# Attention stage of an audio tower kernel: another order of the softmax and query work in a step

## What is computed

```
q = rmsnorm(rope(x @ wq.T)) * q_norm_w        # 16 heads, x is the layer norm of h
k = rmsnorm(rope(x @ wk.T)) * k_norm_w        # 1 head
v = x @ wv.T
attn = softmax(mask(q @ k.T / 8))             # causal, 128 rows by 128 columns, per head
h = h + (attn @ v) @ wo.T
rmsnorm(x) = x * rsqrt(mean(x * x over the 64 values) + eps)
```

## Time and profile before

| | |
|---|---|
| time, median of 3 runs | 1922.25 us (1918.28 to 1922.78) |
| the profiled execution, its own time | 1921.04 us |
| its span | 1919.1 us |
| TensorE matmul (PE) busy | 1778.8 us, 93% |
| TensorE weight load (PEld) busy | 1275.9 us, 66% |
| VectorE (DVE) busy | 1530.7 us, 80% |
| ScalarE (ACT) busy | 1355.5 us, 71% |
| GpSimd (POOL) busy | 920.5 us, 48% |

### The profile page before, as it was taken

How to read it: one execution, slowest core, us unless ns; L and a number is a source line. 1 busy time by engine, 2 the same in 40 slices (tenths; PEclk the granted TensorE clock), 3 DMA queues, 4 the chain that set the end, 5 groups by cost and what they waited for, 6 DMA issues and landing times.

```text
span 1919.1 us, 35529 instructions
## 1 busy us (share of the span) xinstructions
PE 1778.8 (93%) x10789; PEld 1275.9 (66%) x10789; DVE 1530.7 (80%) x3377; ACT 1355.5 (71%) x3865; POOL 920.5 (48%) x1544
## 2 busy tenths in 40 slices
PE   3999999999999977999997999999999999989998
PEld 2777887887887866877775666666655665654443
DVE  5788888888888856567657899998999888986665
ACT  1567777677677653444445999999998999986765
POOL 1222322322322310032238999999898999983200
PEclk9999999999999988999997999999999999999999
DMA  3311111111111000000000000000000000004454
GB/s 98 95 44 40 34 45 39 34 45 39 34 45 39 25 1 1 1 1 1 1 1 1 2 2 2 2 2 2 2 2 1 2 2 2 2 7 177 189 216 165
DMA packets 30520, 69.05 MB, mean 36 GB/s; under 512 B 14108, under 2 KB 14748, under 8 KB 28028
## 3 DMA queue, kind: packets, MB, share of 16 engines
q1 hardware_dynamic: 30332, 66.78, 10.6%
HBM read 45.12 MB, written 2.36 MB: 25 GB/s over the span
## 4 chain that ended last, share of the span: by engine, by line
PE 33%; DVE 10%; ACT 9%; issue 6%; POOL 4%; DVEq 0%; ACTq 0%; POOLq 0%
ACT apb L1460 5%; PE ps L65 4%; PE ps L67 3%; PE ps L66 3%; PE ps L1218 3%; PE ps L1777 3%; PE ps L1201 3%; PE ps L1189 3%; PE ps L1228 2%; POOL apb L1574 1%; DVE atq L1281 1%; PE ps L1763 1%; PE ps L1184 1%; DVE amx L1321 1%; ACT aqT L1449 1%
## 5 line engine op out<-in xcount | busy, mean ns | idle before, releaser
L1460 ACT ACTIVATE apb<-ps,amx 128x128 f32<-128x128 f32 x1024 | 360.5, 369 | 23.6 <-DVE amx L1321 22.8
L1574 POOL TENSOR_TENSOR apb<-apb,arc 128x512 f32<-128x512 f32 x256 | 268.2, 1048 | 28.4 <-DVE arc L1329 27.4
L1460 ACT ACTIVATION_READ_ACCUMULATOR apb<-ps,amx 128x1 f32 x1024 | 214.4, 209 | 0.0
L1336 DVE COPY apT<-ps 128x512 f32<-128x512 f32 x256 | 172.6, 674 | 51.2 <-PE ps L1201 47.9
L583 POOL TENSOR_TENSOR h0h<-h0h,const 128x1 fp32r<-128x1 f32 x256 | 46.7, 218 | 338.8 <-DVE h0l L479 338.8
L65 PE MATMUL ps<-h0h,w123h 128*128 128x512 f32 x512 | 203.2, 397 | 0.0
L67 PE MATMUL ps<-h0h,w123l 128*128 128x512 f32 x512 | 202.5, 396 | 0.0
L66 PE MATMUL ps<-h0l,w123h 128*128 128x512 f32 x512 | 202.5, 395 | 0.0
L479 DVE SCALAR_TENSOR_TENSOR h0l<-ps,h0h 128x1024 fp32r<-128x1024 f32 x128 | 156.1, 1219 | 46.5 <-ACT h0h L383 46.5
L1201 PEld LDWEIGHTS ps<-const,apb 128*128 128x128 f32 x1024 | 109.8, 141 | 121.3 <-issue 90.9
L1321 DVE TENSOR_REDUCE amx<-ps 128x4 f32<-128x512 f32 x256 | 174.3, 681 | 4.6 <-PE ps L1189 4.3
(11 more groups left out here) (325 smaller groups left out, 5030.8 us busy)
## 6 DMA issues: line engine op xcount, KB each, us to landing
h<-gates SPq DMA_DIRECT2D x8, 2048.0 KB, 7.0
atq<-gates SPq DMA_DIRECT2D x8, 2048.0 KB, 7.0
x0k<-x0h SPq DMA_DIRECT2D x128, 72.0 KB
x<-in_x SPq DMA_DIRECT2D x32, 192.0 KB, 2.6
x0k<-x0l SPq DMA_DIRECT2D x64, 72.0 KB
x0k<-x0h SPq DMA_DIRECT2D x64, 48.0 KB
out<-akT SPq DMA_DIRECT2D x16, 128.0 KB, 1.9
x0k<-x0l SPq DMA_DIRECT2D x32, 48.0 KB
```

What stands on the lines that cost most here:

```text
L1336: ve.tensor_copy(pT[:, 4 * k:4 * k + 4, :], ps[:, TB, :].rearrange("p (h t) -> p h t", h=4)).then_inc(S["pT"], 1)
L1460: last = ac.activation(pb[:, i % 2, head, :], ps[:, SB[n % 3], h * T:(h + 1) * T], ACT.Exp, bias=mx[:, k, h:h + 1], accum_out=sm[:, i % 2, ...
L1574: po.tensor_tensor(p, p, rc[:, i % 2, 4 * k:4 * k + 4].unsqueeze(2).to_broadcast([T, 4, T]), ALU.mult).then_inc(S["pn"], 1)
```

## The change

- Slots of `rms_q` and `scale_q`: `rms_q` is called once per item, over all 16 heads, in slot `4 i - 7`. `scale_q` comes two slots later than before, one slot ahead of `q_t`.
- `square` reads the rotated sum `qr` from SBUF (and waits for `add_q`), no longer the bank QB. So `project`, which overwrites QB, waits for the rotation and not for the square.
- VectorE: in an even slot both maxima of the step; in an odd slot `recip(u - 1)`, `rope_q`, `recip(u)`, `sum_q` (two slots after its `rope_q`), then `p_copy`.
- ScalarE: in an odd slot `exps(u)` comes first; in an even slot `exps(u)` comes after the copies and ahead of `keep_x` and `square`.

```diff
-    at_rms = by_slot(HALVES, lambda m: 4 * (m // 2) - 9 + 2 * (m % 2))
-    at_qm = by_slot(HALVES, lambda m: 4 * (m // 2) - 8 + 2 * (m % 2))
+    at_rms = by_slot(B, lambda i: 4 * i - 7)
+    at_qm = by_slot(HALVES, lambda m: 4 * (m // 2) - 6 + 2 * (m % 2))
...
             if m >= 1:
-                pe.wait_ge(S["sq"], m)
+                pe.wait_ge(S["rope"], m)
...
             if i >= 1:
-                ve.wait_ge(S["lrq"], m - 1)
+                ve.wait_ge(S["lrq"], i)
...
-            if 0 <= u < PARTS:
-                maximum(u)
-            if 0 <= u - 1 < PARTS:
-                recip(u - 1)
+            if u % 2 == 0:
+                if 0 <= u < PARTS:
+                    maximum(u)
+                    maximum(u + 1)
+            else:
+                if 0 <= u - 1 < PARTS:
+                    recip(u - 1)
+                if u in at_q:
+                    rope_q(at_q[u])
+                if 0 <= u < PARTS:
+                    recip(u)
+                if u - 2 in at_q:
+                    sum_q(at_q[u - 2])
             if u in at_pt:
                 p_copy(at_pt[u])
-            if u in at_q:
-                rope_q(at_q[u])
-            if u - 1 in at_q:
-                sum_q(at_q[u - 1])
...
-            ac.wait_ge(S["rope"], m + 1)
+            ac.wait_ge(S["qr"], m + 1)
             if i >= 1:
                 ac.wait_ge(S["ssq"], m - 1)
-            ac.activation(sqb[:, h, :], ps[:, QB, :], ACT.Square).then_inc(S["sq"], 1)
-
-        def rms_q(m):
-            i, h = m // 2, m % 2
-            heads = slice(8 * h, 8 * h + 8)
-            ac.wait_ge(S["ssq"], m + 1)
-            ac.activation(lrq[:, heads], ssq[:, heads], ACT.Ln, bias=epsc[:, 1:2], scale=1.0 / DH
-                          ).then_inc(S["lrq"], 1)
-            ac.wait_ge(S["lrq"], m + 1)
+            ac.activation(sqb[:, h, :], qr[i % 2][:, h, :], ACT.Square).then_inc(S["sq"], 1)
+
+        def rms_q(i):
+            ac.wait_ge(S["ssq"], 2 * i + 2)
+            ac.activation(lrq[:], ssq[:], ACT.Ln, bias=epsc[:, 1:2], scale=1.0 / DH).then_inc(S["lrq"], 1)
+            ac.wait_ge(S["lrq"], i + 1)
             if i >= 1:
-                ac.wait_ge(S["qm"], m - 1)
-            ac.activation(rq[:, heads], lrq[:, heads], ACT.Exp, scale=-0.5).then_inc(S["rq"], 1)
+                ac.wait_ge(S["qm"], 2 * i)
+            ac.activation(rq[:], lrq[:], ACT.Exp, scale=-0.5).then_inc(S["rq"], 1)
...
+            if u % 2 == 1 and 0 <= u < PARTS:
+                exps(u)
             if u - 1 in at_pv:
                 keep_o(at_pv[u - 1])
-            if u - 1 in at_q:
-                square(at_q[u - 1])
             if u - 1 in at_qt:
                 keep_q(at_qt[u - 1])
             if u in at_rms:
                 rms_q(at_rms[u])
-            if u in at_xt:
-                keep_x(at_xt[u])
...
-            if 0 <= u < PARTS:
+            if u % 2 == 0 and 0 <= u < PARTS:
                 exps(u)
+            if u in at_xt:
+                keep_x(at_xt[u])
+            if u - 1 in at_q:
+                square(at_q[u - 1])
...
-            po.wait_ge(S["rq"], m + 1)
+            po.wait_ge(S["rq"], m // 2 + 1)
```

## The result

The changed kernel takes 2002.27 us (median of 4 runs, 1998.03 to 2003.35) against 1921.39 us for the kernel before, timed beside it: ratio 1.0419, 95% interval 1.0399 to 1.0439. It is 81 us slower. The forecast was 1972 us, +50; the result lies 0.7 us inside the upper end of the range of 1926 to 2003.

The account below looks back on a forecast made before the run. A new ring of VectorE and ScalarE waits was to bind each attention step at 5.46 us. Groups of 43.68 + 2.55 + 0.2 + 0.2 = 46.63 us against 43.30 gave +46.6, the tail +4: 1972 us, range 1926 to 2003.

Parts of the forecast that it names:

- the ring: VectorE and ScalarE, attention steps: maximum, exponentials(e), square, exponentials(o), reciprocal(o), `p_copy`, `sum_q`, next maximum; 5.46 us per step; chance 0.72.
- a fall of the clock in every group: TensorE in the step with `statistics`: idling lowers its clock, +1.6 us per group, +23 in all, 1995 us; chance 0.08.
- What is put into the ring: VectorE and ScalarE: `residual` 0.79, `statistics` 0.93, `keep_x` 0.50, `sum_k` 0.33 lengthen their steps, 2.55 us per group.
- Scores have 1.9 us in hand, and the excess of 2 x 0.51 goes into that: TensorE in the two `w_o` steps: spare time before scores absorbs their excess; 0.2 us per group, ends 0 and 1.0.
- the transposes ahead of `p_copy` have less in hand: TensorE in the `w_o` steps: these transposes have less spare time than scores; 0.2 us per group taken.
- Bounded by that 0.5 us of slack turning into 0 to 0.3 per step: GpSimd: cost if it fell behind with `add_q` or the later `scale_q`; 0 to 0.3 us per step.
- The square from SBUF at 0: ScalarE: square reading SBUF instead of PSUM changes the step by -0.03 to +0.06 us; taken at 0.
- The ends: Outside the 14 regular groups: nothing ahead of 1057 us, +4 us in the 63 us behind, ends 0 and 10.
- The saved pair and the `project` wait at nothing: ScalarE's saved Ln and Exp lie in a gap, and TensorE was not late by `project`'s wait; no gain from either.
- Faster: VectorE reaches reciprocal(o) after its exponentials end, so no wait binds there; 1902 us; chance 0.12.
- No change: Attention steps: 5.36 us, with `residual`, `statistics` and `keep_x` finding cover; 1924 us; chance 0.07.
- The clock falling in every step: TensorE: idling lowers its clock in every step, 112 times +4.7 us, up to 2500 us; chance 0.01.

Follow-up runs that it names:

- the edit that puts 0.5 us into it: Changed kernel with `keep_o` ahead of the exponentials in odd slots: 2039.85 us, ratio 1.0626.
- `scale_q` first: Changed kernel with `scale_q` ahead of `normalize` in GpSimd's order, nothing else: 1988.81 us, ratio 1.0353.
- the pair per half: Changed kernel with the root-mean-square pair again once per half item, pair and scaling in the slots of before: 1988.76 us, ratio 1.0359.
- both rings open, `keep_o` first: Changed kernel, odd reciprocal a slot later, `keep_o` ahead of odd exponentials, plus pair once per half item (1937.06 us) or `scale_q` ahead of `normalize` (1942.36 us).

## Why the forecast was right, and why too small

The direction and the mechanism held. That the time fell inside the range was luck: the ring's own range ended at 1996, and what lies above was room for a fall of the clock in every group, which came in one. The 30.3 us that were missing are in terms taken too small, below.

**The ring: right, in five of the eight steps.** 5.44 against 5.46, and the edit that puts 0.5 us into it lengthens the steps by that. In the steps with `rope_k` and `w_o` other things last longer: VectorE's own list and TensorE's matmuls.

**What is put into the ring: right.** `residual` with `keep_y`, `statistics`, `keep_x`, `sum_k`: 6.47, 6.39, 5.95, 5.79 against 6.45, 6.39, 5.96, 5.79. `rope_k` was costed at nothing and took 0.08: in that step the reciprocals no longer wait, and VectorE's own list is 5.54 long. That `sum_k` came out to the hundredth in the group shown is partly chance, for the reason given under the table; in the groups where its reciprocals wait it takes 5.78 or 5.79 too.

**"Scores have 1.9 us in hand, and the excess of 2 x 0.51 goes into that": this step failed.** The term was 0.2 per group and measured 1.10 (6.04 + 5.98 - 2 x 5.46). Its upper end, 1.0, was nearer. Half of it is the next point's doing: with `scale_q` first the two steps take 5.51 and 5.97, 0.56 over the ring. (Scores do not start 2.25 us after the maximum there, but 4.19: 1486.34 to 1490.53.) For the other half the prediction had the reason in words ("the transposes ahead of `p_copy` have less in hand") but took the lower price: the `p_t` behind `w_o` comes late, the even slot's `p_copy` waits for it (1.58 and 1.51 us in the steps at 1486.34 and 1492.38), and both reciprocals, `rope_q` and the next maximum are queued behind that. This is read from the trace and was not tried by itself, and a rival stands beside it. With `scale_q` first, `p_v` ahead of `w_o` waited 0.38 us for `keep_o` (1480.36), with the pair per half 0.87 (1481.93), so `keep_o` behind the exponentials can make `w_o` late as well. With both rings open, `keep_o` first shortened the first `w_o` step, from scores to scores, from 6.85 to 5.97 us.

**"Bounded by that 0.5 us of slack turning into 0 to 0.3 per step", taken at 0: failed.** `scale_q` made `q_t` wait 55 us in the stretch of the earlier trace rows. I had weighed GpSimd's busy time (39.39 of 43.29 us) and not the order in its queue: it was not short of time, but `scale_q` stood behind a `normalize` that waits for the ring's reciprocal. In most steps TensorE made that up. Ahead of `w_o` it could not:

```profile
1483.57 0.63 PE L1169 MATMUL ps<-const,atq 128*128 128x128 f32 x4 [1.75 <-POOL atq L1571]
1484.56 0.39 PE L1184 MATMUL ps<-maskb,maskt 64*128 64x256 bf16 x4
```

`q_t` is 1.75 us late, and two steps full of matmuls, 5.97 us each, start from there. Loosened alone, it gives back 0.58 per group, 7.5 us in 13 groups, and 13.5 us in all.

**The square from SBUF at 0: nearly.** Its record went from 599 ns to 644, and its time in the queue from 0.50 to 0.52. The Trainium skill ("Perfetto Trace Analysis", "Optimizing Scalar/DVE Operations") has 42 ns between the two memories and calls that engine-busy time. The 45 ns between the records here are as large; the 0.02 us from start to start, which is what the ring felt, are less.

**The ends: too small.** The stage's start and its first 11 steps lost 9.4 us where I had one group's 3.3; the last 12 steps and what follows 12.5 where I had 4. With 13 groups at 0.97 (12.6 us) and 3.0 in disturbed groups this makes 30.3 of missing time, against 80.9 - 50.6. The experiments say little on the ends: loosening `scale_q` by the pair per half moved the first 11 steps by 1.7 us and the last 12 by 1.3. The clock has some part in them: after had 0.57 in 1055 to 1060 us, where before had 1.00, and 0.66 or 0.67 in three stretches of 5 us in the last 12 steps, where before had one, that of the earlier trace rows. How much of the time that is was not worked out.

**The saved pair and the `project` wait at nothing: right.** The wait went, TensorE did not gain; ScalarE, busy 18.5 us less, waits instead.

**Rivals.** Faster: fell, reciprocals waited for exponentials 111 times in the stretch's 96 steps. No change: fell. The clock falling in every step or once per group: fell, 1.00 in the regular group. It did fall in two places before 1700 us, below, and in one of them without any other disturbance: the eight steps from the scores at 1321.49 took 49.18 us, 1.6 over the others, the price that the rival had put on a fall. The forecast had called the `statistics` step (4.3 of 6.4 us busy) "between" its two rows, 3.88 of 5 and 4.49 of 5.72. It is not: those two have nearly the same busy share, 78%, and the step has less, 67%.

**What I said the profile would show.** From maximum to maximum, plain steps 5.4 to 5.5, the growth with `residual` and `statistics`, the two waits: as said, but for the size of the first (78.3 us, not 60) and for the reciprocals of the `rope_k` and `w_o` steps, which find their exponentials ready. That was one of my signs of being wrong, and it holds for both reciprocals in 38 of 96 steps. Wrong: `w_o` steps "no longer at 5.97" (they stayed), and TensorE idle before scores (0.6 us in the stretch). Of the transposes it idled before `q_t` (55.4 us) and not `p_t` (0.2), and before `p_v`, that is, behind the copies and scalings whose place in a queue the change had moved, `keep_o` among them, which I had not costed. By the table of steps that last one cost nothing outside the `w_o` steps.

## What to carry to other kernels

Write down, for each moved instruction, what it stands behind in its new queue and who stands behind its consumer, and follow that round until it closes: a ring is found this way and then priced to a few hundredths from start-to-start times, while busy shares say nothing of it. Price the second-longest ring too, since it takes over once the first is opened, and an edit that opens one ring can cost more than it saves. A slack may be spent once: two terms that each "go into" the same spare time need one account.

## What was not expected of the hardware

TensorE's granted clock is no fixed function of the waits that these rows show. In the changed kernel `q_t` waits 1.73 to 1.78 us once in nearly every group (11 times from 1102 to 1700 us). Ten times the clock stayed at 1.00 through it. Once, with the same wait and the same work ahead of it, it did not:

```profile
1338.93 0.87 PE L1169 MATMUL ps<-const,atq 128*128 128x128 f32 x4 [1.75 <-POOL atq L1571]
...
1340.99 1.82 PE L1189 MATMUL ps<-akT,aqT 64*128 64x128 f32 x16
```

The four transposes took 0.87 us instead of 0.63, and the 16 products of the scores 1.82 instead of 1.06; the clock was 0.74 from 1340 to 1345. In a second place a fill of 1.81 us on GpSimd, for the experts, stood ahead of a `normalize` and so delayed `scale_q`, and `q_t` waited 2.66 us:

```profile
1639.40 1.81 POOL L2083 MEMSET wpool<- 128x2048 f32 x1
...
1645.59 0.63 PE L1169 MATMUL ps<-const,atq 128*128 128x128 f32 x4 [2.66 <-POOL atq L1571]
...
1647.99 1.91 PE L1189 MATMUL ps<-akT,aqT 64*128 64x128 f32 x16
```

From 1640 to 1645 TensorE was busy 2.93 us at 1.00; from 1645 to 1650 the clock was 0.66, partly its lower level of 1.2 GHz, and the 16 products took 1.91 us. That group took 50.53 us.

By the Trainium skill ("TensorE: Matmul & The Clock Gate", section "A second HAM failure mode: psum-queue depth-cycling") frequent short idling between groups of matmuls made the clock of one kernel go back and forth. The regular groups here, TensorE idle for 15% of them, do not bear that out. The kernel with one pair per item alone is nearer to it: TensorE waited 1.8 and 2.1 us before `q_t` in the round shown, and the clock fell and rose again in every regular group.
